# Eight-stage decoder kernel on one core: bit-quantised feed-forward stage with its gate and value biases accumulated on TensorE

## The chip, the cores and the metric

The kernel runs on one core of one Trainium2 chip. The metric is the device time in microseconds of one execution, the median of three executions of the kernel before.

## What is computed

The program runs a four-layer decoder on x (32 sequences of 64 tokens, 256 wide): eight stages, each adding a gated result to x. Only the sixth, called "bit", is touched. It is a feed-forward layer whose three linear layers use integers from -128 to 127 for the tokens and -1, 0, 1 for the weights:

```python
def bit_linear(x, w, b):
    gamma_x = clip(max(abs(x), axis=-1), 1e-5)
    x_dq = clip(round(x * 127 / gamma_x), -128, 127) * gamma_x / 127
    gamma_w = clip(mean(abs(w)), 1e-5)
    w_dq = clip(round(w / gamma_w), -1, 1) * gamma_w
    return x_dq @ w_dq.T + b
gate = silu(bit_linear(x, gate_w, gate_b))      # 256 -> 1024
val = bit_linear(x, val_w, val_b)               # 256 -> 1024
out = bit_linear(gate * val, out_w, out_b)      # 1024 -> 256
```

The integers of a token times the integers of the weights are summed in PSUM. The sum has to be multiplied by the token's scale and the weights' gamma, and the bias is added to that.

## The kernel before

There is one program for each of the five engines; they meet at semaphores, and the order on each engine is the order in which the code is written. x stays in SBUF as 16 tiles of 128 tokens. A stage goes over them in 4 blocks of 4 tiles; in the bit stage a tile t has two halves f of 512 hidden columns each, numbered n = 2t + f within the block.

**TensorE** (`bit_tensor`). `turn` (L1626) transposes the block's integer tokens, `gate_value` (L1613) makes half n of gate and value with 4 matmuls of 512 columns (L1622) into the bank pair n mod 3, and `out_proj` (L1634) transposes the integers of the hidden tile (L1639) and multiplies them with the output weights (L1648). In a block the order is: halves 2, 3, 4, out_proj of tile 0, halves 5, 6, out_proj 1, half 7, out_proj 2, then `turn` and halves 0 and 1 of the next block, then out_proj 3. TensorE waits before a half until the half three places back has been read out of its bank pair.

**VectorE** (`bit_vector`). `gate_value` (L1733) takes both banks of a half out of PSUM, each with one instruction: times the token's scale (`tok_scale`), plus the bias, which lies broadcast over all partitions in `gb_b` (L1742). `to_ints` (L1746) turns the product of a hidden tile into integers: a maximum (L1753), three small operations, a multiply with rounding (L1757), a subtract (L1760). `finish` (L1762) adds the output to x (L1767). After tile 0 the layernorm of the next block follows (`normalise`, ending with L157), after tile 2 its quantisation (`quantise`, L1103 to L1112) and then the token scales (L1778).

**ScalarE** (`bit_scalar`) applies Silu to the gate in SBUF (L1684) and copies transposed integers from PSUM to SBUF (L1679, L1690). In its order both Silus of a tile t stand ahead of the copy for tile t - 1, except for tile 0 of the next block, whose Silus stand behind the copy for tile 3.

**GpSimd** (`bit_gpsimd`) multiplies gate and value into `bh` (L1719) and once a block adds the output bias to x (L1724).

**SyncE** loads the raw weights and biases long before, while the second stage runs (`bit_sync`). The weights' gammas are made in the first block of the third stage, the convolution (`bit_prep_vector`, L1563).

Of the kernel before, what the change touches and what calls it, by code (L numbers as in the profile page):

```python
# [60 lines left out]
def flamingo_kernel(nc, a, out):  # L61
    ctx = ExitStack()
    with ctx:
# [1036 lines left out]
        def quantise(link, src, mid, dst, factor, least, qs=qs, top=None):  # L1100
# [447 lines left out]
        def bit_sync(sp):  # L1548
# [4 lines left out]
            for dst, n, w in ((gb_b[:, 0, :], "gb2", FF2), (gb_b[:, 1, :], "vb2", FF2), (ob_b, "ob2", DIM)):  # L1553
                sp.dma_start(dst, a[n].rearrange("(o n) -> o n", o=1).broadcast_to([P, w])).then_inc(bit_b_in, 16)
# [32 lines left out]
        bv, at = part(work, at, [P, 2, 512])  # L1587
# [22 lines left out]
        def bit_tensor(pe, ph):  # L1610
            pe.wait_ge(bit_w_ready, 3)

            def gate_value(b, t, f, before=None):  # L1613

                n = 2 * t + f
                if n >= 3:
                    pe.wait_ge(bv_ready, 8 * b + n - 2)
                elif before is not None:
                    pe.wait_ge(bv_ready, 8 * before + (7, 8, 6)[n])
                for k in range(2):  # L1620
                    for c in range(KC):
# [872 lines left out]
```

## Time and profile before

| | us |
|---|---|
| three executions | 1728.65, 1729.23, 1737.1 |
| median | 1729.23 |
| the profiled execution, its own time | 1737.16 |
| its span in the profile | 1735.4 |
| bit stage: first transpose at | 998.1 |
| bit stage: last instruction of VectorE on x ends at | 1174.1 |

The profiled execution's time is 7.9 us over the median; the third execution of the three is as long. Busy shares over the whole span are 74% for TensorE, 62% for VectorE, 26% for ScalarE and 18% for GpSimd, but each stage has limits of its own, so the rows below are from the bit stage, and its times are microseconds from the span's start.

### The profile page before, as it was taken

The page shows a single profiled execution, that of the slowest core. Times are in us where ns is not written, and L with a number is a line of the kernel's source. Part 1 is how long each engine was busy: PE and PEld are TensorE (multiplying, and loading weights), DVE is VectorE, ACT ScalarE, POOL GpSimd, SP SyncE. Part 2 cuts the span into 40 slices and gives each one's busy share as a digit, 9 for nine tenths or more (in the row PEclk, how much of TensorE's full clock was granted, in tenths as well). Part 3 has the DMA queues.
Part 4 walks back from the last instruction along what each step waited for, and adds up shares of the span by engine and source line. Part 5 has one row for each costly group of instructions (what it writes and reads, how often), then busy time and mean ns, then how long its engine had stood idle before and what let it go on. Part 6 is the DMA issues. An engine that isn't in the chain of part 4 may idle for free.

```text
span 1735.4 us, 20241 instructions
## 1 busy us (share of the span) xinstructions
PE 1288.0 (74%) x6664; PEld 724.3 (42%) x6670; DVE 1071.7 (62%) x2575; ACT 455.5 (26%) x632; POOL 307.6 (18%) x287
## 2 busy tenths in 40 slices
PE   0011899999979989967767445554888889899997
PEld 0000545454434456635544322221444444455554
DVE  8988435454353356657767778884777778743222
ACT  1124212222203133322232122220443434451110
POOL 2111000000013500023344222223231222200000
PEclk9995799999989999988897666665998989899999
DMA  9000000002000010011110000002222222200001
GB/s 302 12 12 12 1 0 0 0 0 100 1 19 0 0 61 0 1 25 25 24 23 1 5 14 0 0 0 72 75 74 75 75 74 73 75 2 1 0 0 48
DMA packets 67473, 55.73 MB, mean 32 GB/s; under 512 B 23888, under 2 KB 60624, under 8 KB 67152
## 3 DMA queue, kind: packets, MB, share of 16 engines
q1 hardware_dynamic: 66768, 54.67, 10.5%
q8 instruction: 33, 0.54, 0.1%
q10 hardware_dynamic: 640, 0.26, 0.1%
q14 instruction: 32, 0.26, 0.0%
HBM read 39.97 MB, written 14.68 MB: 31 GB/s over the span
## 4 chain that ended last, share of the span: by engine, by line
PE 48%; DVE 19%; issue 13%; DMA 8%; POOL 6%; ACT 2%; SPq 2%; DVEq 0%; POOLq 0%; ACTq 0%
PE banks L1004 6%; PE banks L623 5%; PE banks L406 5%; PE banks L402 5%; DMA sb_work<-scratch 4%; DMA scratch<-sb_work 3%; PE banks L837 3%; PE banks L1011 3%; POOL sb_work L1429 3%; PE banks L829 3%; PE banks L413 2%; PE banks L417 2%; DVE sb_work L317 2%; PE banks L1622 1%; PE banks L1995 1%
## 5 line engine op out<-in xcount | busy, mean ns | idle before, releaser
L2233 DVE TENSOR_REDUCE sb_work<-banks 128x2 f32<-128x512 f32 x256 | 164.6, 686 | 60.6 <-PE banks L1960 56.3
L2103 ACT ACTIVATE sb_work<-banks 128x1024 f32<-128x1024 f32 x128 | 130.8, 1024 | 169.1 <-PE banks L1981 169.0
L523 DVE TENSOR_TENSOR sb_work<-sb_work,banks 128x512 f32<-128x512 f32 x72 | 49.4, 686 | 120.2 <-ACT sb_work L490 120.2
L1429 POOL TENSOR_TENSOR sb_work<-sb_work,sb_consts 128x512 f32<-128x512 f32 x64 | 66.8, 1074 | 270.0 <-ACT sb_work L1377 232.2
L1004 PE MATMUL banks<-sb_work,sb_shelf 128*128 128x512 f32 x256 | 114.4, 592 | 0.0
L623 PE MATMUL banks<-sb_work,sb_ctx_nat 128*64 128x512 f32 (+15 forms) x512 | 89.9, 510 | 7.8 <-DVE sb_work L685 7.8
L406 PE MATMUL banks<-sb_work,sb_shelf 128*128 128x512 f32 (+1 forms) x192 | 88.8, 611 | 8.6 <-DVE sb_work L566 8.6
L1960 PE MATMUL banks<-sb_work 48*128 48x256 bf16 x512 | 64.3, 295 | 41.2 <-DMA sb_work<-scratch 31.3
L1083 DVE TENSOR_TENSOR sb_work<-sb_work,banks 128x512 f32<-128x512 f32 x32 | 22.0, 688 | 110.3 <-ACT sb_work L1069 110.3
L490 ACT ACTIVATE sb_work<-banks 128x512 f32<-128x512 f32 x72 | 42.9, 596 | 178.2 <-PE banks L402 116.2
L980 POOL TENSOR_TENSOR sb_late<-sb_w2n 128x1024 f32<-128x1024 f32 x10 | 22.7, 2267 | 368.4 <-DVE sb_work L677 367.8
L402 PE MATMUL banks<-sb_work,sb_shelf 128*128 128x512 f32 (+1 forms) x192 | 84.9, 593 | 0.0
L230 PE MATMUL banks<-sb_ident,sb_work 128*128 128x128 f32 x32 | 7.9, 427 | 92.6 <-DVE sb_work L319 92.6
L1995 PE MATMUL banks<-sb_work,sb_late 128*64 128x256 f32 x512 | 75.5, 419 | 0.2
L1995 PE MATMUL banks<-sb_work,sb_shelf 128*64 128x256 f32 x512 | 72.0, 403 | 0.0
L1004 PEld LDWEIGHTS banks<-sb_work,sb_shelf 128*128 128x128 f32 x256 | 48.6, 190 | 49.2 <-issue 47.8
L837 PE MATMUL banks<-sb_wpr,sb_work 128*128 128x256 f32 x256 | 61.9, 388 | 6.9 <-DVE sb_work L916 6.9
L829 PE MATMUL banks<-sb_work,sb_wgu 128*128 128x512 f16 x256 | 63.2, 395 | 2.5 <-DVE sb_work L898 2.5
L1639 PE MATMUL banks<-sb_ident_h,sb_work 128*128 128x128 bf16 x128 | 16.3, 305 | 62.5 <-DVE sb_work L1760 62.5
L623 PEld LDWEIGHTS banks<-sb_work,sb_ctx_nat 128*64 128x64 f32 x512 | 36.0, 136 | 60.8 <-issue 45.0
L1719 POOL TENSOR_TENSOR sb_work<-sb_work 128x512 f32<-128x512 f32 x32 | 40.3, 1269 | 118.7 <-ACT sb_work L1684 118.5
L1960 PEld LDWEIGHTS banks<-sb_work 48*128 48x128 bf16 x512 | 18.3, 96 | 102.3 <-DVE sb_work L2233 38.5
(285 smaller groups left out, 2604.9 us busy)
## 6 DMA issues: line engine op xcount, KB each, us to landing
sb_work<-scratch SPq DMA_DIRECT2D x64, 192.0 KB
scratch<-sb_work SPq DMA_DIRECT2D x32, 192.0 KB, 2.3
sb_work<-ctx_t SPq DMA_DIRECT2D x16, 256.0 KB, 4.5
scratch<-sb_work SPq DMA_DIRECT2D x32, 128.0 KB, 2.2
sb_work<-ctx_t SPq DMA_DIRECT2D x4, 512.0 KB, 3.6
sb_ctx_nat<-ctx SPq DMA_DIRECT2D x1, 2048.0 KB, 11.4
sb_raw<-wguT SPq DMA_DIRECT2D x1, 2048.0 KB, 15.7
scratch<-sb_work SPq DMA_DIRECT2D x32, 64.0 KB, 1.9
```

Source lines behind the costliest of these rows:

```text
L402: ins = nc.tensor.matmul(dst[0:ms, :], w[:, c, m0:m0 + ms], moe_xT[:, c, :], start=c == 0, stop=c == KC - 1, skip_group_check=True)
L406: ins = nc.tensor.matmul(dst[0:ms, :], w[:, m0:m0 + ms], zz[:, k, :], start=False, stop=True, skip_group_check=True)
L623: ins = nc.tensor.matmul(o, ctx_nat[:, tap, g * SEQ:(g + 1) * SEQ], xg[:, g, :, l0 + 1 + 2 * tap:SEQ + 1 + 2 * tap], start=tap == TILES - ...
L829: ins = nc.tensor.matmul(bank[2 * (m % 2) + half], wgu[:, c, half * FF1 + m * P:half * FF1 + (m + 1) * P], xs[:, c, :], start=c == 0 and n ...
L837: ins = nc.tensor.matmul(bank[4 + t // 2][:, (t % 2) * DIM:(t % 2 + 1) * DIM], h1[:, m % 4, t * P:(t + 1) * P], wpr[:, m, :], start=m == 0 ...
L1004: ins = nc.tensor.matmul(bank[2 * (m % 2) + half], w[:, c, m * P:(m + 1) * P], xT3[:, c, :], start=c == 0, stop=c == KC - 1)
L1011: ins = nc.tensor.matmul(bank[4 + t // 2][:, (t % 2) * DIM:(t % 2 + 1) * DIM], h3[:, m % 4, t * P:(t + 1) * P], w2hT[:, m, :], start=m == ...
L1429: ins = nc.gpsimd.tensor_tensor(km_[:, hf, k, :, :], keys.unsqueeze(1).broadcast_to([P, 8, SEQ]), hm2.unsqueeze(2).broadcast_to([P, 8, SEQ ...
L1960: ins = nc.tensor.matmul(bank[u % 2][:, h * C3:(h + 1) * C3], qS[rows, i, 2 * hp + h, tc * P:(tc + 1) * P], kS[rows, i, 2 * hp + h, :], st ...
L1995: ins = nc.tensor.matmul(bank[6][k * SEQ:(k + 1) * SEQ, u * C3:(u + 1) * C3], vv3[j][:, sc_, 2 * k + u, a_ * VW3:(a_ + 1) * VW3], pt3[:, h ...
L2103: nc.scalar.activation(pt3[:, h % 2, :, :], o, ACT.Exp).then_inc(exp3, 1)
L2233: nc.vector.tensor_reduce(out=mx3[:, tc, k, 2 * hp:2 * hp + 2], in_=bank[u % 2].rearrange("p (h s) -> p h s", h=2), axis=AX, op=ALU.max).t ...
```

## The change

Gate and value no longer get their biases on VectorE. The bias is divided by the weights' gamma once, while the convolution runs, and split into three bf16 pieces (on VectorE, seven instructions); six small DMAs lay the pieces as six rows `b_rows`. For each block GpSimd splits 1/scale of the tokens (`qr`) into three bf16 pieces, six columns `r_parts`; TensorE transposes them (4 transposes to 6 partitions), ScalarE copies them to `r_rows`. One more matmul of 6 rows by 512 columns in each bank then adds bias/(scale x gamma) to the sum (6 pairs of pieces), so that a multiplication by the token's scale alone gives the biased value. Silu reads PSUM with the token's scale as its multiplier, and VectorE makes value x scale x gate in one instruction into `bh`. GpSimd has no products left.

```diff
@@ quantise
+            if scales is not None:
+                for k in range(2):
+                    nc.vector.tensor_scalar(scales[:, k, :], qs[:, :], gam[:, k:k + 1], None, ALU.mult)
             for t in range(BT):
                 ins = nc.vector.tensor_scalar(mid[:, t, :], src[:, t, :], qr[:, t:t + 1], ROUND, ALU.mult, ALU.add)
...
@@ bit_sync, bit_rows (called after attn2_sync)
-            for dst, n, w in ((gb_b[:, 0, :], "gb2", FF2), (gb_b[:, 1, :], "vb2", FF2), (ob_b, "ob2", DIM)):
-                sp.dma_start(dst, a[n].rearrange("(o n) -> o n", o=1).broadcast_to([P, w])).then_inc(bit_b_in, 16)
+            for k, n in enumerate(("gb2", "vb2")):
+                sp.dma_start(b_flat[k * SEQ:(k + 1) * SEQ, :], a[n].rearrange("(p n) -> p n", p=SEQ)).then_inc(bit_b_in, 16)
...
+        def bit_rows(sp):
+            sp.wait_ge(b_split, 1)
+            for j, (_, piece) in enumerate(SPLITS2):
+                sp.dma_start(b_rows[j:j + 1, :, :].rearrange("p k n -> p (k n)"), b_parts[:, piece, :]).then_inc(bit_b_in, 16)
...
@@ bit_prep_vector
+            dve.wait_ge(gam_ready, 1)
+            dve.wait_ge(bit_b_in, 48)
+            for k in range(2):
+                v = b_flat[k * SEQ:(k + 1) * SEQ, :]
+                link(nc.vector.tensor_scalar(v, v, gamr[k * SEQ:(k + 1) * SEQ, k:k + 1], None, ALU.mult))
+            for piece in range(3):
+                ins = nc.vector.tensor_copy(b_parts[:, piece, :], b_flat)
+                if piece < 2:
+                    link(ins)
+                    link(nc.vector.tensor_tensor(b_flat, b_flat, b_parts[:, piece, :], ALU.subtract))
...
@@ bit_tensor, gate_value
                 if n >= 3:
-                    pe.wait_ge(bv_ready, 8 * b + n - 2)
+                    pe.wait_ge(bh_ready, 8 * b + n - 2)
...
+                if n == 0:
+                    pe.wait_ge(b_intT_ready, 2 * b + 2)
+                for k in range(2):
+                    ins = nc.tensor.matmul(bank[2 * (n % 3) + k], r_rows[:, t * P:(t + 1) * P],
+                                           b_rows[:, k, f * 512:(f + 1) * 512], start=False, stop=True)
                 ins.then_inc(b_gv, 1)
@@ bit_tensor, turn
                 ins.then_inc(b_turned, 1)
+                pe.wait_ge(r_parts_ready, b + 1)
+                pe.wait_ge(b_intT_ready, 2 * b + 1)
+                for t in range(BT):
+                    ins = nc.tensor.transpose(bf_bank(6)[0:len(SPLITS2), t * P:(t + 1) * P], r_parts[:, t, :], ident_h[:, :])
+                ins.then_inc(b_turned, 1)
@@ bit_scalar
+                act.wait_ge(b_turned, 2 * b + 2)
+                nc.scalar.activation(r_rows, bf_bank(6)[0:len(SPLITS2), 0:BTOK], ACT.Copy).then_inc(b_intT_ready, 1)
...
-                    act.wait_ge(bg_ready, 8 * b + 2 * t + f + 1)
-                    nc.scalar.activation(bg[:, f, :], bg[:, f, :], ACT.Silu).then_inc(b_silu, 1)
+                    n = 2 * t + f
+                    if n >= 2:
+                        act.wait_ge(bh_ready, 8 * b + n - 1)
+                    elif before is not None:
+                        act.wait_ge(bh_ready, 8 * before + n + 7)
+                    act.wait_ge(b_gv, 8 * b + n + 1)
+                    nc.scalar.activation(bg[:, f, :], bank[2 * (n % 3)], ACT.Silu,
+                                         scale=tok_scale[:, 0, t:t + 1]).then_inc(b_silu, 1)
@@ bit_gpsimd
+            def inverse_parts(b):
+                pool.wait_ge(b_int_ready, b + 1)
+                one = ones[:, 0:1].unsqueeze(2)
+                link(nc.gpsimd.tensor_tensor(r_parts[:, :, 0:3], qr[:, :].unsqueeze(2).broadcast_to([P, BT, 3]),
+                                             one.broadcast_to([P, BT, 3]), ALU.mult))
+                link(nc.gpsimd.tensor_tensor(r_rest, qr[:, :], r_parts[:, :, 0], ALU.subtract))
...
+            inverse_parts(0)
             pool.wait_ge(ob_ready, 1)
-                        nc.gpsimd.tensor_tensor(bh[:, t % 2, f * 512:(f + 1) * 512], bg[:, f, :], bv[:, f, :],
-                                                ALU.mult).then_inc(bh_ready, 1)
...
+            with pool.Fori(0, BLOCKS - 1) as b:
+                link.enter(b, 3)
+                pool.wait_ge(x_done, updated(ph, b))
+                xs = x[:, bass.ds(BT * b, BT), :]
+                nc.gpsimd.tensor_tensor(xs, xs, ob_b.unsqueeze(1).broadcast_to([P, BT, DIM]),
+                                        ALU.add).then_inc(ob_added, 1)
+                inverse_parts(b + 1)
...
@@ bit_vector, gate_value is now gated, at the same places
-                    dve.wait_ge(b_gv, 8 * b + n + 1)
-                    for k, (dst, done) in enumerate(((bg, bg_ready), (bv, bv_ready))):
-                        nc.vector.scalar_tensor_tensor(
-                            out=dst[:, f, :], in0=bank[2 * (n % 3) + k], scalar=tok_scale[:, k, t:t + 1],
-                            in1=gb_b[:, k, f * 512:(f + 1) * 512], op0=ALU.mult, op1=ALU.add).then_inc(done, 1)
+                    dve.wait_ge(b_silu, 8 * b + n + 1)
+                    nc.vector.scalar_tensor_tensor(
+                        out=bh[:, t % 2, f * 512:(f + 1) * 512], in0=bank[2 * (n % 3) + 1],
+                        scalar=tok_scale[:, 1, t:t + 1], in1=bg[:, f, :], op0=ALU.mult, op1=ALU.mult).then_inc(bh_ready, 1)
```

**TensorE from out_proj of tile 2 over the end of a block's loop round.** A row is an instruction; REGISTER_ALU and ISA rows set up waits, x8 counts equal neighbours. Before:

```order
L1648 MATMUL banks<-sb_late,sb_work 128x256 x8
L1627 REGISTER_ALU
L1630 MATMUL banks<-sb_ident_h,sb_work 128x128 x8
L1619 REGISTER_ALU
L1622 MATMUL banks<-sb_late,sb_work 128x512 x4
L1619 REGISTER_ALU
L1622 MATMUL banks<-sb_late,sb_work 128x512 x4
L1635 REGISTER_ALU
L1639 MATMUL banks<-sb_ident_h,sb_work 128x128 x8
```

The same place with the change:

```order
L1686 MATMUL banks<-sb_late,sb_work 128x256 x8
L1660 REGISTER_ALU
L1663 MATMUL banks<-sb_ident_h,sb_work 128x128 x8
L1667 ISA
L1669 MATMUL banks<-sb_ident_h,sb_work 6x128 x4
L1647 REGISTER_ALU
L1650 MATMUL banks<-sb_late,sb_work 128x512 x4
L1653 REGISTER_ALU
L1655 MATMUL banks<-sb_late,sb_work 128x512 x2
L1647 REGISTER_ALU
L1650 MATMUL banks<-sb_late,sb_work 128x512 x4
L1655 MATMUL banks<-sb_late,sb_work 128x512 x2
```

Four transposes stand between the turn and the first half, and each half has two more matmuls; nothing else changes place.

**ScalarE at the same place**, with the change: L1735 copies hidden integers, L1716 the token integers, L1718 the new rows, L1728 is Silu.

```order
L1716 ACTIVATE sb_work<-banks 128x1024
L1717 REGISTER_ALU
L1718 ACTIVATE sb_work<-banks 6x512
L1732 REGISTER_ALU
L1735 ACTIVATE sb_work<-banks 128x1024
L1727 ISA
L1728 ACTIVATE sb_work<-banks,sb_tok_scale 128x512
L1727 REGISTER_ALU
L1728 ACTIVATE sb_work<-banks,sb_tok_scale 128x512
```

The copy L1718 is new. The two Silus of the next block's tile 0 still stand behind the copy of tile 3, and they now are what empties the gate's banks.

## Rows read from the trace of the kernel before

**Rows 1.** Windows: us; busy (x) of PE, PEld, DVE, ACT, POOL; clock; DMA; GB/s.

```profile
998.00:1174.10 176.10, 88.20 (x410) 47.15 (x416) 138.99 (x325) 40.81 (x53) 49.34 (x36) 0.64 0.01 3
```

**Rows 2.** Waits, 1004 to 1174: who waited for whom, us in total, times, longest.

```profile
DVE sb_work L1742 <- PE banks L1622: 18.8, 12, 4.2
```

**Rows 3.** Timeline, end of a block: start, us, engine, line, what, [idle before <- releaser].

```profile
1038.78 0.69 DVE L1112 TENSOR_SCALAR sb_work<-sb_work 128x1024 bf16<-128x1024 f32 x1
...
1039.59 1.06 PE L1630 MATMUL banks<-sb_ident_h,sb_work 128*128 128x128 bf16 x8
...
1041.84 3.59 PE L1622 MATMUL banks<-sb_late,sb_work 128*128 128x512 bf16 x8 [1.19 <-ACT sb_work L1679]
...
1045.22 0.70 PE L1639 MATMUL banks<-sb_ident_h,sb_work 128*128 128x128 bf16 x8
...
1047.12 1.04 PE L1648 MATMUL banks<-sb_late,sb_work 128*128 128x256 bf16 x8 [1.19 <-ACT sb_work L1690]
1048.00 2.75 PE L1622 MATMUL banks<-sb_late,sb_work 128*128 128x512 bf16 x12
...
1051.71 1.21 DVE L1753 TENSOR_REDUCE sb_work<-sb_work 128x1 f32<-128x1024 f32 x1
```

**Rows 4.** Timeline, tile 0 and layernorm of the next block.

```profile
1053.62 1.77 DVE L1757 TENSOR_SCALAR sb_work<-sb_work 128x1024 f32<-128x1024 f32 x1
1055.42 0.69 DVE L1760 TENSOR_SCALAR sb_work<-sb_work 128x1024 bf16<-128x1024 f32 x1
...
1056.17 1.04 PE L1639 MATMUL banks<-sb_ident_h,sb_work 128*128 128x128 bf16 x8 [5.42 <-DVE sb_work L1760]
...
1062.44 2.72 DVE L1742 SCALAR_TENSOR_TENSOR sb_work<-banks,sb_tok_scale,sb_late 128x512 f32<-128x512 f32 x4
1065.08 1.20 DVE L1753 TENSOR_REDUCE sb_work<-sb_work 128x1 f32<-128x1024 f32 x1
```

**Rows 5.** Timeline, tiles 1 and 2, to the next block's integers.

```profile
1066.95 0.75 DVE L1757 TENSOR_SCALAR sb_work<-sb_work 128x1024 f32<-128x1024 f32 x1
1067.74 0.69 DVE L1760 TENSOR_SCALAR sb_work<-sb_work 128x1024 bf16<-128x1024 f32 x1
...
1070.72 1.89 PE L1648 MATMUL banks<-sb_late,sb_work 128*128 128x256 bf16 x8 [1.19 <-ACT sb_work L1690]
...
1074.35 1.41 DVE L1742 SCALAR_TENSOR_TENSOR sb_work<-banks,sb_tok_scale,sb_late 128x512 f32<-128x512 f32 x2 [4.20 <-PE banks L1622]
1075.67 1.21 DVE L1753 TENSOR_REDUCE sb_work<-sb_work 128x1 f32<-128x1024 f32 x1
...
1082.18 0.69 DVE L1112 TENSOR_SCALAR sb_work<-sb_work 128x1024 bf16<-128x1024 f32 x1
```

**Rows 6.** Groups by line and form: xcount | busy us, mean ns | idle before, releaser.

```profile
L1377 ACT ACTIVATE sb_work<-banks,sb_shelf 128x512 f32<-128x512 f32 x8 | 5.1, 684 | 32.5 <-PE banks L1327 32.5
```

**Rows 7.** The same view, GpSimd.

```profile
L2169 POOL TENSOR_TENSOR sb_work<-sb_work,sb_ones 128x256 bf16<-128x256 f32 x32 | 19.6, 614 | 212.5 <-DVE sb_work L2217 117.5 <-DMA sb_work<-scratch 95.0
L1724 POOL TENSOR_TENSOR sb_x<-sb_x,sb_late 128x1024 f32 x4 | 9.4, 2354 | 0.0
```

**Rows 8.** Timeline, first block of the convolution, after the gammas.

```profile
529.31 1.97 PE L613 MATMUL banks<-sb_ident,sb_work 128*128 128x128 f32 x16 [0.46 <-DVE sb_late L1567]
```

**Rows 9.** Windows (columns as in rows 1) in two stretches of rows 3.

```profile
1041.00:1045.00 4.00, 3.16 (x8) 1.19 (x9) 3.83 (x9) 0.71 (x1) 0.00 (x0) 0.50 0.01 2
1045.50:1048.60 3.10, 1.91 (x19) 1.35 (x17) 1.67 (x3) 2.06 (x3) 1.02 (x1) 1.00 0.00 0
```

**Rows 10.** Timeline, TensorE one block later; and matmuls of 48 rows in the next stage.

```profile
1085.24 3.59 PE L1622 MATMUL banks<-sb_late,sb_work 128*128 128x512 bf16 x8 [1.19 <-ACT sb_work L1679]
1088.62 1.06 PE L1639 MATMUL banks<-sb_ident_h,sb_work 128*128 128x128 bf16 x8
1090.87 1.04 PE L1648 MATMUL banks<-sb_late,sb_work 128*128 128x256 bf16 x8 [1.19 <-ACT sb_work L1690]
...
L1960 PE MATMUL banks<-sb_work 48*128 48x256 bf16 x512 | 64.3, 295 | 41.2 <-DMA sb_work<-scratch 31.3 <-DVE sb_work L2233 9.7
```

More of the change, by code:

```diff
@@ L1098, in flamingo_kernel, with quantise @@
         qr = sb("qr", [P, BT])
-        def quantise(link, src, mid, dst, factor, least, qs=qs, top=None):
+        def quantise(link, src, mid, dst, factor, least, qs=qs, top=None, scales=None):
             link(nc.vector.tensor_reduce(out=amax[:, :], in_=src, axis=AX, op=ALU.max, apply_absolute_value=True))
@@ L1528, in flamingo_kernel @@
         ATTN2_LINKS = 17
+        SPLITS2 = ((0, 0), (0, 1), (0, 2), (1, 0), (1, 1), (2, 0))
         gwT, at = part(late, 0, [P, 2, KC, FF2], BF16)
         owT, at = part(late, at, [P, MC, DIM], BF16)
-        gb_b, at = part(late, at, [P, 2, FF2])
+        b_rows, at = part(late, at, [len(SPLITS2), 2, FF2], BF16)
+        b_flat, at = part(late, at, [P, 2 * FF2 // P])
+        b_parts, at = part(late, at, [P, 3, 2 * FF2 // P], BF16)
         ob_b, at = part(late, at, [P, DIM])
@@ L1586, in flamingo_kernel @@
         bg, at = part(work, at, [P, 2, 512])
-        bv, at = part(work, at, [P, 2, 512])
+        r_rest, at = part(work, at, [P, BT])
+        r_parts, at = part(work, at, [P, BT, len(SPLITS2)], BF16)
+        r_rows, at = part(work, at, [len(SPLITS2), BTOK], BF16)
         bh, at = part(work, at, [P, 2, FF2])
@@ L1616, in gate_value @@
                 if n >= 3:
-                    pe.wait_ge(bv_ready, 8 * b + n - 2)
+                    pe.wait_ge(bh_ready, 8 * b + n - 2)
                 elif before is not None:
-                    pe.wait_ge(bv_ready, 8 * before + (7, 8, 6)[n])
+                    pe.wait_ge(bh_ready, 8 * before + (7, 8, 6)[n])
                 for k in range(2):
                     for c in range(KC):
-                        ins = nc.tensor.matmul(bank[2 * (n % 3) + k], b_intT[:, c, t * P:(t + 1) * P],
-                                               gwT[:, k, c, f * 512:(f + 1) * 512], start=c == 0, stop=c == KC - 1)
+                        nc.tensor.matmul(bank[2 * (n % 3) + k], b_intT[:, c, t * P:(t + 1) * P],
+                                         gwT[:, k, c, f * 512:(f + 1) * 512], start=c == 0, stop=False)
+                if n == 0:
[3 more added lines that the diff above has]
+                                           b_rows[:, k, f * 512:(f + 1) * 512], start=False, stop=True)
                 ins.then_inc(b_gv, 1)
@@ L1700, in block_ @@
                 if not last:
-                    silu(b + 1, 0)
+                    silu(b + 1, 0, before=b)
             ints(0)
@@ L1773, in ints @@
                 if not isinstance(b, int):
-                    dve.wait_ge(b_turned, b)
-                quantise(link, xn[:, :, :], b_mid, b_int, 1.0 / 127.0, 1e-5, top=True).then_inc(b_int_ready, 1)
-                dve.wait_ge(b_int_ready, b + 1)
-                for k in range(2):
-                    link(nc.vector.tensor_scalar(tok_scale[:, k, :], qs[:, :], gam[:, k:k + 1], None, ALU.mult))
+                    dve.wait_ge(b_turned, 2 * b)
+                quantise(link, xn[:, :, :], b_mid, b_int, 1.0 / 127.0, 1e-5, top=True,
+                         scales=tok_scale).then_inc(b_int_ready, 1)
             def block_(b, last):
                 for t in range(1, BT):
-                    gate_value(b, t)
+                    gated(b, t)
                     to_ints(b, t - 1)
@@ L1793, in block_ @@
                 if not last:
-                    gate_value(b + 1, 0, before=b)
+                    gated(b + 1, 0)
                 finish(b, BT - 1)
             ints(0)
-            gate_value(0, 0)
+            gated(0, 0)
             with dve.Fori(0, BLOCKS - 1) as b:
@@ L2340, in _ @@
             attn2_sync(sp, PHASE["attn2"])
+            bit_rows(sp)
             sp.wait_ge(bit_w_ready, 3)
```

43 lines of the change are left out of this document (19 added, 24 removed).

## The prediction

> **What bounds the kernel now.** I read the windows view of the bit stage first. Of its 176.1 us VectorE is busy for 139.0 and TensorE for 88.2, at a granted clock of 0.64 in the mean, so TensorE works mostly at 1.2 GHz (0.5) and at times at 2.4 GHz (1.0) [rows 1]. Neither engine is full. The waits say where VectorE stands still: 12 times, 18.8 us in all and up to 4.2 us at once, for the matmuls of a half [rows 2]. The timeline of one block then shows who leads where. A block lasts 43.4 us (the integers of the next block are done at 1038.78 + 0.69 = 1039.47 and at 1082.18 + 0.69 = 1082.87) [rows 3, 5]. I cut it at four events on VectorE, the reductions that begin tiles 0, 1 and 2, and the integers:
>
> - A, integers to reduction 0: 1039.47 to 1051.71, 12.2 us. A chain over TensorE and ScalarE: turn, copy, 8 wide matmuls, transposes, copy, output matmuls, then wide matmuls and evictions [rows 3].
> - B, to reduction 1: 1065.08, 13.4 us. VectorE alone: to_ints, layernorm, four evictions [rows 4].
> - C, to reduction 2: 1075.67, 10.6 us. to_ints on VectorE, then transposes, copy, output matmuls and half 7 on TensorE, then two evictions, of which 4.20 us are a wait [rows 5].
> - D, to the integers: 1082.87, 7.2 us. VectorE alone [rows 5].
>
> So taking 32 instructions from VectorE pays only in B, and whatever is put on TensorE or ScalarE is paid in A and C. The rest of the argument is the size of these four.
>
> **Prices.** A wide matmul costs (3.59 - 0.2)/8 = 0.425 us at 1.2 GHz and (2.75 - 0.17)/12 = 0.215 at 2.4 (the 0.2 is my estimate of the last one's tail) [rows 3]. The new matmul streams the same 512 columns from 6 rows instead of 128. The trace has none like it; I take the full price, since nothing in the rows shows that fewer rows save time. Its lower bound is nothing, its upper one the same 0.425. If it were free, A would lose 1.9 us, C 0.85 and B nothing, and the sum would be some 9 us better. The Trainium skill, "TensorE: Matmul & The Clock Gate", section "Why this matters for your kernels", says that one matmul over 32 rows takes as long as one over 128; by it the full price stands and the thin rows are no discount for this change. No row here shows 6 rows. A transpose costs (1.06 - 0.2)/8 = 0.107 us at 1.2 GHz [rows 3]. Silu from PSUM with a scale read from SBUF: the nearest row reads 128x512 from PSUM with such an operand, 684 ns [rows 6]. Handing over from engine to engine I put at 0.05 us, and 0.19 from TensorE. The product reads a bank and SBUF as the eviction did, (2.72/4 = 0.68 in a row, 0.74 alone) [rows 4].
>
> **A: +1.5 us.** After the turn come 4 transposes, 4 x 0.107 = 0.43, so the wide matmuls begin at 1041.84 + 0.43 = 1042.27. They are 12 instead of 8. The clock rose at about 1045.3 before, since 1041 to 1045 shows 0.50 and 1045.5 on shows 1.00 [rows 9]; I let it rise at the same time. Then 7 of them run at 0.425 and 5 at 0.215 and end at 1046.3, against 1045.2: +1.1 for the transposes of tile 3, which now start at 1046.3 and not at 1045.22. The copy on ScalarE (1.02) ends at about 1048.05. The Silus of halves 0 and 1 stand behind that copy on ScalarE, although their matmuls are long done; they and the copy end at 1049.4. Meanwhile TensorE does the output matmuls from 1047.12 + 1.1 = 1048.2, and after 8 of them (0.9) half 2, 6 x 0.215 = 1.3, and half 3, another 1.3: until 1051.7. Then 0.17, Silu 0.68, 0.05 and the product 0.70: reduction 0 at 1053.25 instead of 1051.71. Nothing of the copy to `r_rows` shows: it runs under the first 4 wide matmuls (1.7 us), and its cost is at most that of a copy of 128 partitions, below the 0.68 of rows 6. The four small GpSimd operations have the 2.37 us from the integers to the wide matmuls; a 128x256 operation there takes 0.61 [rows 7] and these have at most 12 columns, so between 0 and 4 x 0.61 = 2.4 us, and I take the low end: 0.
>
> **B: -2.0 us.** GpSimd's product held up the multiply of tile 0: it took 1.77 us against 0.75 for the same instruction in tile 1 [rows 4, 5]. That is 1.0 us per block gone. Its place could be taken by GpSimd's addition to x (2.35 us) [rows 7], but that starts once the last tile's update is through, about 1050.8, and ends before the multiply (1055.2). to_ints then takes 4.40 - 1.02 = 3.38 us and the layernorm 1062.44 - 1056.11 = 6.33 [rows 4]. Product 4 follows (0.74). Product 5 waits for its Silu: output chain 4.17 us (1068.43 to 1070.72 + 1.88) [rows 5], then 6 wide matmuls of which the last run at 2.4 GHz (2.1), and 0.19 + 0.05 + 0.68 + 0.05: 3.38 + 4.17 + 2.1 + 0.97 = 10.6 after reduction 0, the product done at 11.35. So TensorE takes over here by 0.2 us: 11.4 instead of 13.4. Three evictions went away (2.0) and one wait came.
>
> **C: +0.6 us.** Chain 3.35 + 4.17 + 6 x 0.425 + 0.97 + 0.70 = 11.7 instead of 10.6: +1.15 at 1.2 GHz. But TensorE's bursts in B and C are half as long again, so part of it may run at 2.4 GHz, and then it would be about 0. I take the middle.
>
> **D: +0.3 us.** The two token scales (0.49 us for both before, behind the integers) now stand ahead of the integers; they overlap neighbours a little.
>
> Sum of a block: 1.5 - 2.0 + 0.6 + 0.3 = +0.4 us, four blocks +1.6. Outside the stage: in the convolution seven small VectorE operations of some 0.2 us, 1.5 us with their waits, stand ahead of the next copies, which need 16 transposes of 1.97 us first [rows 8], so 0. If that cover were gone it would cost 1.5, once. SyncE's six DMAs go out where its queue waits for nothing urgent, more than 400 us before their use; two broadcasts of 0.5 MB each disappear. The profiled execution took 1737.16 us, so by this sum 1738.8; the median of the executions shown is 7.9 lower, and I carry the difference over: 1729.2 + 1.6 = 1730.8, call it **1731 us**. Its own range is 1726 to 1736.
>
> **Rivals.**
>
> 1. *TensorE stays at 1.2 GHz.* Slower. The rise at 1045.3 came behind a dense burst. If thin matmuls and transposes do not keep TensorE active as the wide ones do, the bursts of A are diluted by a third and the rise doesn't come. Then A pays 5 x 0.21 for the wide matmuls, 0.35 for the transposes, 0.85 for the output matmuls and 12 x 0.21 for halves 2 and 3: +4.8; B pays 0.4 and C the other 0.55. That is up to 5.7 per block, 23 in all, but the first block hardly starts otherwise than before, so 15 to 20: 1746 to 1751, 1748 in the middle. It decides from the point where more than half of the blocks lose their rise (8.65 us are 0.5%). Against it: one block later 8 wide matmuls ended slow (3.59), the transposes behind them too (1.06), and the output matmuls then ran fast (1.04), so transposes seem to help; and 48 rows run at 295 ns in the next stage [rows 10]. For it: nothing here has 6 rows. The Trainium skill, the same page, section "Part 4: PE-mode transpose", says that transposes don't count as activity in the same way; by it this rival is likelier, and rows 10 speak against it as far as transposes go. Chance 0.20.
> 2. *TensorE stays at 2.4 GHz.* Faster. Longer bursts and shorter gaps may hold the clock up. Then C takes 1.5 + 0.6 less than I said, A 2.1 less (7 wide matmuls and the turn), B 0.95 less: 5 per block, 20 in all, 1711; half of it gives 1721. Against it: in a gap of some 5 us after half 4 the clock fell in each block, and the gap that is left is still 3 to 4 us. Chance 0.15.
> 3. *The stall doesn't go.* The change frees the multiply only if GpSimd's addition or its new small operations don't meet it. If they do, B is -1.0: +4 in all, 1735. Chance 0.07, for the times above keep them 2 us apart.
>
> **How the numbers follow.** Forecast 0.56, rivals 0.20, 0.15, 0.07, and 0.02 for what I don't see. About 0.5%, 8.65 us, is what a measurement of this kernel can tell from no change. Faster by more: rival 2, and one hundredth, 0.16. Slower by more: rival 1 and one hundredth, 0.21. The same: 0.63. The range reaches from 1722 to 1748: it leaves out rival 2, which is 0.15, and the upper end of rival 1.
>
> **What would show it.** Right: VectorE's busy time in the stage falls by some 26 us (32 x 0.69, and 4 x 1.0 of the stall) while the stage stays near 177 us; the multiply takes 0.75 us in all tiles; VectorE's waits change from TensorE to Silu and about double; a block is 43 to 45 us, with A near 13.8, B 11.4, C 11 and D 7.5. Wrong: a granted clock far from 0.64 in the stage (rivals 1 and 2), a new matmul much shorter than 0.2 us apart, `r_rows` later than the fourth wide matmul, or a wait in the convolution.

## The result, and the profile after

| | before | after |
|---|---|---|
| median, us (17 runs each) | 1731.8 | 1751.01 |
| lowest to highest | 1720.2 to 1737.74 | 1740.67 to 1760.5 |
| the profiled execution, its span | 1735.4 | 1745.9 |
| its bit stage, first integers to last update | 176.2 | 191.3 |

The ratio is 1.0109, with the interval 1.009 to 1.0129: slower by 19 us. The forecast was no change, 1731; the result is above the range of 1722 to 1748, at the upper end of what rival 1 gave (1746 to 1751). Here is the windows view of the stage after (columns as in rows 1), then of two stretches within it:

```profile
994.50:1185.80 191.30, 127.07 (x496) 50.94 (x496) 113.64 (x292) 44.56 (x57) 12.70 (x20) 0.59 0.01 3
997.40:1011.40 14.00, 13.97 (x31) 2.77 (x30) 4.28 (x6) 4.62 (x6) 0.68 (x1) 0.50 0.01 2
1086.50:1104.00 17.50, 16.31 (x48) 4.75 (x46) 5.22 (x8) 4.14 (x6) 2.34 (x1) 0.50 0.00 0
```

VectorE is rid of 25.35 us of work (138.99 to 113.64), as forecast (26). TensorE's busy time rose from 88.20 to 127.07, far more than 64 matmuls at 0.215 to 0.425 (13.8 to 27.2) account for, and the granted clock fell from 0.64 to 0.59. The second and third row are two stretches in which TensorE never paused, or hardly (busy for 13.97 of 14.00 us and 16.31 of 17.50), and yet stayed at 0.50, that is 1.2 GHz. The waits view, 1004 to 1186, now puts VectorE's waits thus (columns as in rows 2):

```profile
DVE sb_work L1793 <- ACT sb_work L1728: 61.1, 23, 7.3
DVE sb_x L1818 <- PE banks L1686: 3.7, 2, 3.4
```

18.8 us of waiting for TensorE became 61.1 us for Silu, which in turn stands behind TensorE. The first block of the stage, TensorE in the timeline of before:

```profile
1000.63 6.15 PE L1622 MATMUL banks<-sb_late,sb_work 128*128 128x512 bf16 x19 [1.52 <-ACT sb_work L1679]
```

and TensorE in the same place after:

```profile
997.39 1.89 PE L1650 MATMUL banks<-sb_late,sb_work 128*128 128x512 bf16 x4
...
999.22 1.03 PE L1655 MATMUL banks<-sb_late,sb_work 6*128 6x512 bf16 x2
...
1000.18 1.89 PE L1650 MATMUL banks<-sb_late,sb_work 128*128 128x512 bf16 x4
...
1008.52 1.89 PE L1650 MATMUL banks<-sb_late,sb_work 128*128 128x512 bf16 x4
...
1010.34 1.03 PE L1655 MATMUL banks<-sb_late,sb_work 6*128 6x512 bf16 x2
```

Before, 19 matmuls of 512 columns take 6.15 us, so more than half of them ran at 2.4 GHz. After, five halves follow each other without a gap for 14 us and the last (1008.52) is as slow as the first. There is a second thing to see, for which I had no term. A half begins every 2.79 us (997.39, 1000.18), but six matmuls at 0.425 are 2.55. The missing 0.24 lies at the two changes between 128 rows and 6: the thin pair starts 0.13 late (999.22 instead of 997.39 + 4 x 0.425 = 999.09), the next wide one 0.11 late.

To compare stages block by block I cut them as the prediction did and added up the parts over the blocks (A, B and C four times, D three times, and the end, from reduction 2 of the last block to the last update of x). "First" is the first block's A, "others" the A of blocks 2, 3 and 4.

| kernel | A first | A others | B | C | D | end | stage | clock |
|---|---|---|---|---|---|---|---|---|
| before | 10.2 | 12.2, 12.6, 12.7 | 53.6 | 42.3 | 21.6 | 11.0 | 176.2 | 0.64 |
| after | 15.5 | 12.7, 19.3, 17.8 | 46.3 | 45.5 | 22.4 | 11.8 | 191.3 | 0.59 |
| after, second profile | 15.5 | 17.8, 17.7, 17.7 | 46.7 | 44.7 | 22.4 | 11.8 | 194.4 | 0.59 |
| before, second profile | 10.2 | 12.3, 12.6, 10.6 | 53.6 | 42.0 | 21.6 | 11.8 | 174.7 | 0.66 |

The 15.1 us come from A (+17.6), C (+3.2) and two small parts (+1.6), and B gives 7.3 back. Over two profiles each the stage is 192.9 against 175.5, +17.4, close to the 19 us of the medians. The two can't be subtracted to the microsecond, though, since the time ahead of the stage differs from profile to profile by more than that: the first integers come at 998.0 and 999.8 us before and at 994.5 and 991.5 after.

### The profile page after: what moved, and what is told of

It is laid out like the page before. It is cut to its first block, busy times and chain, and to the rows that moved or that the text cites. A ratio compares the mean times of both kernels' runs of the same rounds, so it can differ in the third digit from the quotient of the medians.

```text
span 1745.9 us, 20322 instructions
## 1 busy us (share of the span) xinstructions
PE 1323.8 (76%) x6750; PEld 729.1 (42%) x6750; DVE 1047.1 (60%) x2550; ACT 458.9 (26%) x636; POOL 270.7 (16%) x271
## 3 DMA queue, kind: packets, MB, share of 16 engines
q1 hardware_dynamic: 67504, 53.65, 10.3%
## 4 chain that ended last, share of the span: by engine, by line
PE 50%; DVE 17%; issue 13%; DMA 8%; POOL 6%; ACT 3%; SPq 2%; DVEq 0%; POOLq 0%; ACTq 0%
PE banks L1004 6%; PE banks L623 5%; PE banks L406 5%; PE banks L402 5%; DMA sb_work<-scratch 4%; PE banks L837 3%; DMA scratch<-sb_work 3%; PE banks L1011 3%; POOL sb_work L1432 3%; PE banks L829 3%; PE banks L413 2%; PE banks L417 2%; PE banks L1650 2%; PE banks L1686 2%; PE banks L2044 2%
## 5 line engine op out<-in xcount | busy, mean ns | idle before, releaser
L623 PE MATMUL banks<-sb_work,sb_ctx_nat 128*64 128x512 f32 (+15 forms) x512 | 88.4, 503 | 7.8 <-DVE sb_work L685 7.8
L490 ACT ACTIVATE sb_work<-banks 128x512 f32<-128x512 f32 x72 | 42.9, 596 | 178.2 <-PE banks L402 116.2
L1793 DVE SCALAR_TENSOR_TENSOR sb_work<-banks,sb_tok_scale,sb_work 128x512 f32<-128x512 f32 x32 | 23.7, 749 | 67.6 <-ACT sb_work L1728 67.6
L2009 PEld LDWEIGHTS banks<-sb_work 48*128 48x128 bf16 x512 | 18.5, 96 | 102.7 <-DVE sb_work L2282 41.1
L623 PEld LDWEIGHTS banks<-sb_work,sb_ctx_nat 128*64 128x64 f32 x512 | 36.6, 134 | 58.6 <-issue 43.1
L1011 PE MATMUL banks<-sb_raw,sb_work 128*128 128x256 f32 x256 | 59.8, 379 | 0.0
```

The lines of the kernel that those rows point to most:

```text
L623: ins = nc.tensor.matmul(o, ctx_nat[:, tap, g * SEQ:(g + 1) * SEQ], xg[:, g, :, l0 + 1 + 2 * tap:SEQ + 1 + 2 * tap], start=tap == TILES - ...
L1011: ins = nc.tensor.matmul(bank[4 + t // 2][:, (t % 2) * DIM:(t % 2 + 1) * DIM], h3[:, m % 4, t * P:(t + 1) * P], w2hT[:, m, :], start=m == ...
L2009: ins = nc.tensor.matmul(bank[u % 2][:, h * C3:(h + 1) * C3], qS[rows, i, 2 * hp + h, tc * P:(tc + 1) * P], kS[rows, i, 2 * hp + h, :], st ...
```

## The experiments

**Theory T.** A matmul over 6 rows takes as long as one over 128, but doesn't help the clock to rise as that does. So bursts in which every third matmul is over 6 rows stay at 1.2 GHz. **Rival B** (R in the first expectations, theory B in that of run 9): the loss is the added matmuls' own time, the 0.11 us at each change of the row count and the longer chain, whatever the clock. **Rival L**: the longer loss is chance of one profile, or lies outside the stage.

**1. The same 64 matmuls over 128 rows.** The 122 further rows of `b_rows` and `r_rows` are zeros.

```diff
-        b_rows, at = part(late, at, [len(SPLITS2), 2, FF2], BF16)
+        b_rows, at = part(late, at, [P, 2, FF2], BF16)
...
+            link(nc.vector.memset(b_rows, 0.0))
...
-        r_rows, at = part(work, at, [len(SPLITS2), BTOK], BF16)
+        r_rows, at = part(work, at, [P, BTOK], BF16)
...
-                nc.scalar.activation(r_rows, bf_bank(6)[0:len(SPLITS2), 0:BTOK], ACT.Copy).then_inc(b_intT_ready, 1)
+                nc.scalar.activation(r_rows[0:len(SPLITS2), :], bf_bank(6)[0:len(SPLITS2), 0:BTOK], ACT.Copy).then_inc(b_intT_ready, 1)
...
+            link(nc.gpsimd.memset(r_rows, 0.0))
```

> The changed kernel with the bias matmuls over 128 rows instead of 6: the other 122 rows are zeros, so the sums and the number of columns stay the same. Theory T (the thin matmuls do not keep TensorE active, so its clock stays at 1.2 GHz): the granted clock of the bit stage goes from 0.54 back to 0.64 or more, the bursts at the block ends rise to 2.4 GHz again, and the time is 1729 to 1737 against 1751. Rival R (the added matmuls cost by their number and their order, whatever their rows): the time stays within 3 us of the changed kernel's and the bursts stay slow.

**2. The bias matmuls left out.** The kernel after without its 64 bias matmuls, so gate and value get no bias; all else (the rows, the transposes, the copies) stays.

```diff
-                    ins = nc.tensor.matmul(bank[2 * (n % 3) + k], r_rows[:, t * P:(t + 1) * P],
-                                           b_rows[:, k, f * 512:(f + 1) * 512], start=False, stop=True)
```

> The changed kernel without the 64 bias matmuls: gate and value get no bias, all else stays, the four small transposes, the copy and the GpSimd pieces too. T: wide matmuls alone raise the clock as before, stage about 170 us, time 1720 to 1728. R: the 64 matmuls took 0.43 us each at 1.2 GHz, about half of them on the path, so 1751 - 14 = 1737, with the clock as slow as in the changed kernel.

**3 and 4. The kernel before with two added matmuls a half**, over 6 or over 128 rows of zeros (`zr[0:128, ...]`), which change no sum. `zr` is filled with zeros at the kernel's start.

```diff
+                for k in range(2):
+                    ins = nc.tensor.matmul(bank[2 * (n % 3) + k], zr[0:6, 0:P], zr[0:6, :], start=False, stop=True)
```

> The kernel before with one thing added: two matmuls of 6 rows of zeros by 512 columns per half, into the same sums. T: the clock falls as in the changed kernel, granted clock of the stage 0.54, time 1748 to 1758. R: only their own time on the path, 2 halves in A and 1 in C, 3 x 0.9 us x 4 blocks at 1.2 GHz or half of it at 2.4: 1736 to 1743.

> The same added matmuls with 128 rows of zeros. T: the clock holds, 0.64 or more, time 1734 to 1741, at least 8 us under the same with 6 rows. R: the same time as with 6 rows.

| kernel | median (executions) | median of before, run beside it | ratio, interval | A first | A others | B | C | stage | clock |
|---|---|---|---|---|---|---|---|---|---|
| 1 after, 128 rows | 1743.87 (9) | 1729.42 | 1.0078, 1.005 to 1.0107 | 11.4 | 14.4, 14.6, 14.6 | 45.5 | 42.9 | 177.6 | 0.70 |
| 2 after, none | 1722.49 (10) | 1729.42 | 0.9948, 0.9921 to 0.9975 | 9.6 | 10.3, 12.3, 12.2 | 44.4 | 42.5 | 165.4 | 0.68 |
| 3 before, + 6 rows | 1745.43 (4) | 1729.42 | 1.0102, 1.0058 to 1.0147 | 14.8 | 12.5, 12.5, 18.9 | 50.2 | 45.3 | 187.7 | 0.61 |
| 4 before, + 128 rows | 1739.52 (10) | 1729.42 | 1.0056, 1.003 to 1.0082 | 11.3 | 14.4, 13.8, 13.5 | 52.3 | 44.6 | 182.6 | 0.70 |

TensorE of run 1 in the timeline, first block:

```profile
1015.72 1.06 PE L1651 MATMUL banks<-sb_late,sb_work 128*128 128x512 bf16 x2
1016.57 1.06 PE L1656 MATMUL banks<-sb_late,sb_work 128*128 128x512 bf16 x2
1017.42 1.58 PE L1651 MATMUL banks<-sb_late,sb_work 128*128 128x512 bf16 x4
...
1019.27 1.03 PE L1651 MATMUL banks<-sb_late,sb_work 128*128 128x512 bf16 x4
1020.13 0.60 PE L1656 MATMUL banks<-sb_late,sb_work 128*128 128x512 bf16 x2
1020.57 1.03 PE L1651 MATMUL banks<-sb_late,sb_work 128*128 128x512 bf16 x4
```

Same number of instructions, same columns, same order: with 128 rows the clock is up within the second half, and from there a half lasts 1.30 us (1019.27 to 1020.57), which is 6 x 0.216, with nothing between the forms. In the other blocks too it rises within the second half or right behind it. The first block's A is 11.4 and not 15.5, all later ones are 14.4 to 14.6, the granted clock of the stage 0.70 instead of 0.59, and the stage 13.7 to 16.8 us shorter. Runs 3 and 4 say the same in the other kernel, without anything else of the change: 6-row matmuls take the rise from the first and the last block (14.8, 18.9), 128-row ones from none. In the two middle blocks of run 3 the clock was up before the burst began, and stayed up. TensorE of run 3 at the end of its first burst is still slow:

```profile
1006.90 1.89 PE L1623 MATMUL banks<-sb_late,sb_work 128*128 128x512 bf16 x4
1008.72 1.03 PE L1626 MATMUL banks<-sb_zr 6*128 6x512 bf16 x2
1009.68 1.89 PE L1623 MATMUL banks<-sb_late,sb_work 128*128 128x512 bf16 x4
1011.50 1.03 PE L1626 MATMUL banks<-sb_zr 6*128 6x512 bf16 x2
```

TensorE of run 4, with 128 rows, is up within its second half:

```profile
1008.98 1.80 PE L1623 MATMUL banks<-sb_late,sb_work 128*128 128x512 bf16 x4
1010.61 0.60 PE L1626 MATMUL banks<-sb_zr 128*128 128x512 bf16 x2
1011.04 1.03 PE L1623 MATMUL banks<-sb_late,sb_work 128*128 128x512 bf16 x4
```

Two 6-row matmuls of zeros a half are thus enough to cost the old kernel 16 us, and over 128 rows they cost 10. The intervals of these two medians overlap; what separates them is the profile, a stage of 187.7 against 182.6. Run 2 gives the whole price of the bias matmuls: without them the changed kernel is 7 us faster than before and its stage some 10 us shorter, with them it is 19 slower.

Theory T named the pattern of the clock rightly, but not the times. Run 1 was expected at 1729 to 1737 and took 1743.87, run 3 at 1748 to 1758 and took 1745.43 (with 0.61 in the stage, not 0.54), and run 4 at least 8 us under run 3, where it was 5.9. (The 0.54 that the expectations give for the kernel after is 0.59 in the windows view.)

What run 1 does not settle: its stage is 1.4 us over before, its median 14.4. With the clock back, 13.7 to 16.8 us of the stage are back, but of the 19 us of the medians only some 5.

**5 to 8. Before once more; ones instead of zeros; another order.** Run 6 fills the 122 further rows of `r_rows` with ones, against rows of zeros in `b_rows`, in case zeros in the stationary operand matter. Runs 7 and 8 aim at the wait in C, which is in both kernels [rows 5]: half 7 is made only behind out_proj 1, though its bank pair is free much earlier. In run 7 (kernel before) TensorE makes halves 2 to 6 in a row:

```diff
-                gate_value(b, 1, 0)
-                for t in range(1, BT):
-                    gate_value(b, t, 1)
-                    if t + 1 < BT:
-                        gate_value(b, t + 1, 0)
-                    out_proj(b, t - 1)
+                for n in range(2, 7):
+                    gate_value(b, n // 2, n % 2)
+                out_proj(b, 0)
+                gate_value(b, 3, 1)
+                out_proj(b, 1)
+                out_proj(b, 2)
```

Run 8 is run 1 with that order, and on ScalarE `silu(b, 1)`, `silu(b, 2)`, `turned(b, 0)`, `silu(b, 3)`, `turned(b, 1)`, `turned(b, 2)`.

> The kernel before, once more, for a second profile: how much stages that no change touches differ from run to run. If the clock's luck is all that differs, the bit stage takes 174 to 180 us and the attention stage ahead of it 188 to 192.

> The 128-row form again, with ones instead of zeros in the 122 stationary rows (the streamed rows stay zero, so the sums are the same). T: as with zeros, stage 177 to 180 us at a clock of 0.64 or more. The time was 1744, which the stage's 177.6 us does not explain; if the longer attention stage ahead of it (199.6 us in that profile against 191) was luck, this run shows 188 to 192 there and a time of 1731 to 1738; if the padding causes it, it is again near 200 and the time near 1744.

> The kernel before with another order on TensorE alone: halves 2 to 6 ahead of out_proj of tile 0, half 7 ahead of out_proj 1. No half then stands behind the transposes of a tile that VectorE has yet to make. If the wait of 4.2 us per block for half 7 is what bounds part C, C falls from 10.6 to about 7, the stage to 162 to 166 us and the time to 1713 to 1720. Rival: the banks are read out too late for the earlier halves, and the time stays at 1729.

> The 128-row form of the changed kernel with the same order on TensorE, and both Silus of tiles 2 and 3 ahead of the copies they do not depend on. C falls to about 6, B loses its wait, A keeps its 14: stage 151 to 157 us, time 1705 to 1720. Rival: VectorE still waits for Silus, since these now wait for its products, and the gain is under half of that.

| kernel | median (executions) | median of before, run beside it | ratio, interval | A first | A others | B | C | stage | clock |
|---|---|---|---|---|---|---|---|---|---|
| 5 before again | 1732.77 (1) | 1733.57 | | 10.2 | 12.3, 12.6, 10.6 | 53.6 | 42.0 | 174.7 | 0.66 |
| 6 128 rows, ones | 1744.96 (12) | 1733.57 | 1.0083, 1.0057 to 1.0108 | 11.3 | 14.0, 14.5, 14.6 | 45.3 | 43.5 | 177.4 | 0.70 |
| 7 before, order | 1715.04 (4) | 1733.57 | 0.9889, 0.9846 to 0.9933 | 10.2 | 12.4, 14.1, 10.6 | 52.6 | 25.2 | 158.5 | 0.63 |
| 8 128 rows, order | 1710.45 (4) | 1733.57 | 0.9881, 0.9835 to 0.9927 | 11.3 | 13.6, 13.8, 14.0 | 44.0 | 20.0 | 151.0 | 0.67 |

Ones or zeros make no difference: stage 177.4 and 177.6. Run 6 was to be at 1731 to 1738 if the long attention stage of run 1 was chance. Its profiled execution was nearly that, 1738.38 with 189.6 us there, but the median of its twelve is 1744.96, near run 1's; so the time that the 128-row form loses outside the stage is no single unlucky execution. The order takes 17.1 us from C alone in the kernel before (42.3 to 25.2, where 28 was expected) and 22.9 in the 128-row form (42.9 to 20.0): C is now VectorE's own work. Its timeline for tile 1 of run 7 shows no gap:

```profile
1062.39 0.69 DVE L1760 TENSOR_SCALAR sb_work<-sb_work 128x1024 bf16<-128x1024 f32 x1
1063.00 0.48 DVE L1767 SCALAR_TENSOR_TENSOR sb_x<-banks,sb_work,sb_x 128x256 f32 x1
1063.40 2.72 DVE L1742 SCALAR_TENSOR_TENSOR sb_work<-banks,sb_tok_scale,sb_late 128x512 f32<-128x512 f32 x4
1066.03 1.21 DVE L1753 TENSOR_REDUCE sb_work<-sb_work 128x1 f32<-128x1024 f32 x1
```

Both beat both kernels. Against before the form of run 8 gains 23, run 7 gains 18.5; their medians differ by 4.6 with overlapping intervals, though the stages differ by 7.5.

**9 to 12. A row count between; 6 rows in the new order; two repeats.** Run 9 has 64 rows instead of 128 (`[64, 2, FF2]`, `[64, BTOK]`). Run 10 is the kernel after with the orders of run 8. Runs 11 and 12 repeat the kernel after and run 1.

> The bias matmuls over 64 rows (6 with data, 58 zeros) instead of 6 or 128. Theory T (TensorE's clock rises only where its work fills rows; 6 rows don't count like 128): a case in between. If 64 rows keep the clock as 128 did, the stage is 177 to 179 us, every block shows a granted clock of 1.00 behind its first halves and the median is 1742 to 1746; if they do it as 6 rows did, stage 187 to 192 and 1749 to 1753, with at least two blocks whose first halves stay at 0.50. Theory B (only the switch between row counts costs, 0.11 us each): a half lasts 2.78 us at 1.2 GHz and 1.50 at 2.4, as with 6 rows, whatever the clock does.

> The change as it is (6 rows) with TensorE's and ScalarE's order of the two kernels before: halves 2 to 6 ahead of out_proj 0. Theory T: the wait in C goes (C near 5 to 7 us instead of 11.2), but the clock is lost in more blocks than with 128 rows, so the stage is 163 to 170 us against 150.9 there, and the median 1722 to 1730. Rival: with bursts this long 6 rows keep the clock as well, stage 151 to 156, median 1710 to 1716.

> The changed kernel once more, for a second profile. Theory T: stage from the first integers to the last update 187 to 195 us (191.3 in the first), with the same pattern: at least two of four blocks reach their first reduction 15 us or more after the integers. Rival L (the first profile was unlucky in the clock): stage 177 to 180, and the time is missing elsewhere.

> The 128-row form once more, for a third profile of it. Its two profiles show stages of 177.6 and 177.4 us, 2 us over the kernel before (174.7 and 176.2), yet its median is 11 to 14 us over. Rival S: a typical stage of it is longer than profiled, 183 to 190, with a block at 0.50. Rival U: the stage is 177 to 178 again and the rest lies ahead of it, first integers done at 1003 us or later against 998.0 and 999.8.

| kernel | median (executions) | median of before, run beside it | ratio, interval | A first | A others | B | C | stage | clock |
|---|---|---|---|---|---|---|---|---|---|
| 9 after, 64 rows | 1739.55 (10) | 1733.15 | 1.0051, 1.0027 to 1.0075 | 12.1 | 14.3, 14.5, 15.0 | 44.2 | 43.6 | 177.9 | 0.70 |
| 10 after, order | 1720.11 (4) | 1733.15 | 0.9923, 0.9894 to 0.9952 | 15.5 | 12.7, 19.3, 17.8 | 44.4 | 19.9 | 163.8 | 0.58 |
| 11 after again | 1750.87 (1) | 1733.15 | | 15.5 | 17.8, 17.7, 17.7 | 46.7 | 44.7 | 194.4 | 0.59 |
| 12 128 rows again | 1747.96 (1) | 1733.15 | | 11.4 | 14.4, 14.6, 14.6 | 45.5 | 42.9 | 177.6 | 0.70 |

Run 9 parts the theory from rival B. Its TensorE, first at the start of a block, then a little later:

```profile
1048.78 1.89 PE L1651 MATMUL banks<-sb_late,sb_work 128*128 128x512 bf16 x4
1050.60 1.03 PE L1656 MATMUL banks<-sb_late,sb_work 64*128 64x512 bf16 x2
1051.57 1.13 PE L1651 MATMUL banks<-sb_late,sb_work 128*128 128x512 bf16 x4
...
1055.85 1.03 PE L1651 MATMUL banks<-sb_late,sb_work 128*128 128x512 bf16 x4
1056.81 0.60 PE L1656 MATMUL banks<-sb_late,sb_work 64*128 64x512 bf16 x2
1057.34 1.04 PE L1651 MATMUL banks<-sb_late,sb_work 128*128 128x512 bf16 x4
1058.31 0.60 PE L1656 MATMUL banks<-sb_late,sb_work 64*128 64x512 bf16 x2
```

The pause at a change of the row count is there as with 6 rows (a half lasts 1.49, 1055.85 to 1057.34, or 2.79), but the clock rises after the first half, as with 128. The stage is 177.9, so the pause costs little by itself and the clock is the stage's loss. (Its median, 1739.55, is below the 1742 to 1746 expected.) In run 10 (median 2 us below the expected 1722 to 1730) C falls to 19.9, and A stays what it is in the kernel after. Beside run 8, the same order over 128 rows, its stage is 12.8 us longer and its median 9.7; no execution of run 8 was above 1716.18, none of run 10 below 1717.09. This is the clearest sign in whole times that the rows matter. In its first block seven halves follow each other at 1.2 GHz without a gap, and in its third TensorE is at 1.2 GHz through all seven halves, 0 and 1, and behind out_proj 3 another five in a row; their first and last in the timeline:

```profile
1082.50 1.89 PE L1650 MATMUL banks<-sb_late,sb_work 128*128 128x512 bf16 x4
...
1091.96 1.92 PE L1650 MATMUL banks<-sb_late,sb_work 128*128 128x512 bf16 x4
...
1103.11 1.89 PE L1650 MATMUL banks<-sb_late,sb_work 128*128 128x512 bf16 x4
1104.92 1.03 PE L1655 MATMUL banks<-sb_late,sb_work 6*128 6x512 bf16 x2
```

Run 11 answers rival L: its stage is 194.4, and in none of its four blocks is the clock up by the second half. TensorE in its second block, from the second half on:

```profile
1043.22 1.89 PE L1650 MATMUL banks<-sb_late,sb_work 128*128 128x512 bf16 x4
...
1049.90 1.91 PE L1650 MATMUL banks<-sb_late,sb_work 128*128 128x512 bf16 x4
1051.75 0.86 PE L1655 MATMUL banks<-sb_late,sb_work 6*128 6x512 bf16 x2
1052.54 1.04 PE L1650 MATMUL banks<-sb_late,sb_work 128*128 128x512 bf16 x4
```

The rise comes at 1052, 12 us after the first half began at 1040.4, and behind transposes, output matmuls and four wide ones, that is behind the part with the fewest 6-row matmuls.

Taken over all runs, a block's matmuls began at 1.2 GHz in 12 blocks with 6 rows (7 of after and run 11, 3 of run 10, 2 of run 3), and in none was the clock up by the end of the second half: in 5 it rose at the end of the third, in 7 not before reduction 0. In each of the 24 blocks with 64 or 128 rows (runs 1, 4, 6, 8, 9, 12) it rose by the end of the second half or right behind it.

Run 12 answers the question left by run 1: the stage is 177.6 again. The rest lies ahead of it. Runs 1 and 12 reach their first integers at 1012.0 and 1012.2, run 6 at 1002.8, before at 998.0 and 999.8, after at 994.5 and 991.5. The windows view of the attention stage that comes ahead of the bit stage (from the first to the last matmul of one line, L1321; columns as in rows 1), of run 12:

```profile
789.60:989.10 199.50, 143.93 (x1000) 100.47 (x1000) 147.71 (x336) 48.10 (x65) 64.31 (x56) 0.80 0.07 16
```

and of run 6:

```profile
790.10:979.70 189.60, 139.37 (x1000) 97.02 (x1000) 140.97 (x336) 48.09 (x65) 64.95 (x56) 0.85 0.08 17
```

The same 1000 matmuls, which the edit doesn't touch, take 10 us more at a clock of 0.80 than at 0.85. In run 1 this stretch takes 199.6, in the other profiles of this study 188 to 195. Why the 128-row form meets the longer one in two of three profiles is open. Ahead of the bit stage its only own instruction is the filling of `b_rows` with zeros, and run 6 differs from run 1 in nothing but a constant; that speaks for a matter of when the stage starts, but no run shows it.

## Why the prediction was wrong

By its own steps:

- **Which parts are bound by what: right.** VectorE lost 25.35 us and the stage did not gain; B alone shortened, C and A paid. VectorE's waits grew from 18.8 to 61.1 us, where "about double" was forecast.
- **A, +1.5: the step that failed.** It said "I let it rise at the same time". In the eight blocks of the two profiles of after it rose in three not at all before reduction 0 (A 15.5, 15.5, 19.3), in four only at the end of the third half (17.7 or 17.8). In one it was up when the burst began, behind the 128-row work of out_proj 2 and the turn, and stayed up through five halves (12.7, under the forecast 13.8): so the 6-row form does not lift the clock, but did not let it fall either. Where the clock rises in all blocks (run 1) A is 11.4, 14.4, 14.6, 14.6, in the sum +7.3 for four blocks against a forecast +6; in the kernel after it is +17.6 and +21.1.
- **Price of the thin matmul, full: right, and short.** Its time per column is that of a wide one: the Trainium skill, "TensorE: Matmul & The Clock Gate", section "Why this matters for your kernels", was drawn on for that, and the runs agree. The change of the row count adds 0.11 to 0.13 us at 1.2 GHz and 0.10 at 2.4 twice a half (2.79 and 1.49 against 2.55 and 1.30), for which the sum had nothing. The sum for a free matmul is off by a slip: 1.9 and 0.85 in four blocks are 11 us, not 9; nothing hangs on it.
- **B, -2.0: right**, 46.3 against 53.6 is -1.8 a block. **The stall is gone:** the multiply takes 0.75 in all 16 tiles [rows 4 had 1.77], and GpSimd's addition (1050.73, 2.36 us) is over before it, as forecast. Rival 3 fell, and so did rival 2 (the clock was 0.59 in the stage, not above 0.64).
- **C, +0.6:** +0.8 (45.5 against 42.3, by 4); +0.1 with 128 rows. **D, +0.3:** +0.3 (22.4 against 21.6, by 3).
- **Costed at nothing, and so it was:** the Silu that reads the gate in PSUM takes 686 ns (684 forecast), the four small GpSimd operations 0.21 each, within the 2.2 us between the integers and the transposes, and the copy of the rows 0.59, beside the first wide matmuls; here the first of them and the copy, in the second block after:

```profile
1040.99 0.21 POOL L1759 TENSOR_TENSOR sb_work<-sb_qr,sb_ones 128x12 bf16<-128x12 f32 x1 [42.90 <-DVE sb_work L1115]
...
1043.43 1.04 PE L1650 MATMUL banks<-sb_late,sb_work 128*128 128x512 bf16 x4
1043.54 0.59 ACT L1718 ACTIVATE sb_work<-banks 6x512 bf16<-6x512 bf16 x1 [0.48 <-PE banks L1669]
```

  The convolution, into which the preparation went, takes 102.3 us after against 103.9 before (first to last matmul of L623).
- **Rival 1, chance 0.20:** the mechanism that came, in A. Its price was 15 to 20 us over the forecast; the stage is 13.5 and 16.6 over the forecast one (177.8), of which A alone has 11.6 and 15.1. The median of 1751.01 against its 1746 to 1751 is in part luck, for before, measured again, is 1731.8 and not 1729.2. Its remark that the first block "hardly starts otherwise" was wrong (10.2 to 15.5). I had weighed rows 10 against it; but the transposes there have 128 rows, and those of 48 rows stand in another stage, between other work. Neither had 6 rows in a third of the burst.
- **The sum, had the clock risen:** +1.6 forecast for the stage, +1.4 measured in run 1 (+2.1 over the mean of both profiles of before). A cost 1.3 more than forecast and C 1.8 less, so that some of the agreement is chance, but one premise decided the sign. It holds for the stage alone: the whole of run 1 is 14.4 us over before, and that rest, ahead of the stage, was neither forecast nor explained.

The chances were at fault too. I took a price from rows of another kind for the time of the matmul, where a bound from both sides held, but a single row for what it does to the clock, where nothing bounded it.

## What to carry to other kernels

A matmul over 6 rows took as long as one over 128, and still the rows mattered: where a burst is what lifts TensorE's clock, keep thin matmuls out of it, or try filling them up with zeros (64 and 128 rows both worked here), and look at the granted clock of the stretch, not at the busy time. The filling mended the stage, not the kernel: with 64 and 128 rows it is still 6 and 11 to 14 us slower than before. Work moved off an engine pays only where that engine is the bound; here the 32 instructions of VectorE bought 7 to 8 us in B, and the added matmuls took them back in A, while the order in which TensorE makes its halves was worth 18 us. When a stage is measured by its effect on the whole, compare it also by itself, since the stages before it move the total: over the 14 profiles the first integers come between 991.5 and 1012.2 us.

## What the runs showed of the hardware

- Matmuls of 512 columns over 6 rows, two beside every four of 128 rows, kept the granted clock at 0.50 through 14 us of unbroken work (after, 997.4 to 1011.4) and 17.5 us of nearly unbroken work (1086.5 to 1104.0: 16.31 busy), and in run 10 through 19.6 us (1007.2 to 1026.8). The same with 64 or 128 rows rose to 1.00 by the end of the second half or right behind it in every block (24 blocks in six profiles). Once up, it stayed up through five halves with 6 rows (after, 1043.4 to 1053.7). The Trainium skill, "TensorE: Matmul & The Clock Gate", section "Part 1: The HAM clock gate (the "warmup" mystery)", says that sustained matmul activity releases the throttle, by time and not by a number of instructions. The 128-row runs are in line with it; in the 6-row ones 14 us of unbroken matmuls did not release it. Between 6 and 64 rows nothing was run.
- The value of the filling doesn't matter: ones or zeros in the further 122 rows of the stationary operand, 177.4 and 177.6 us.
- A change between 128-row matmuls and ones over 6 or 64 rows leaves some 0.1 us unused, at either clock (a half of six takes 2.79 and 1.49 us, with 128 rows throughout 1.30 at 2.4 GHz).
- An unchanged stretch of 1000 matmuls took 189.6 us in run 6 and 199.5 in run 12, with a granted clock of 0.85 and 0.80.
